# A message-passing layer on one core: which nodes a partition of a table step holds

## What is computed

```python
msg_in = concatenate([nodes[row], nodes[col], edge_features], axis=-1)
messages = relu(msg_in @ mW1 + mb1) @ mW2 + mb2
aggregated = segment_sum(messages, col, num_segments=12500)
upd = relu(concatenate([nodes, aggregated], axis=-1) @ uW1 + ub1) @ uW2 + ub2
y = nodes + upd
out = (y - mean(y)) / sqrt(var(y) + 1e-5)     # over the 64 features
```

## Time and profile before

| | us |
|---|---|
| Median of three runs | 2034.05 (2033.94 to 2034.74) |
| The profiled execution's own time | 2035.36 |
| Its span in the trace | 2033.6 |

### The profile page before, as it was taken

How to read it: one execution, slowest core, us unless ns; L and a number is a source line. 1 busy time by engine, 2 the same in 40 slices (tenths; PEclk the granted TensorE clock), 3 DMA queues, 4 the chain that set the end, 5 groups by cost and what they waited for, 6 DMA issues and landing times.

```text
span 2033.6 us, 34717 instructions
## 1 busy us (share of the span) xinstructions
PE 1408.9 (69%) x10080; PEld 1283.7 (63%) x10080; DVE 872.2 (43%) x2225; ACT 557.6 (27%) x928; POOL 1488.3 (73%) x1576
## 2 busy tenths in 40 slices
PE   6777767666667676666766676767676767767775
PEld 6766666566666666666665565656665656656664
DVE  3543333333333333333334444444444444544444
ACT  4322222222222222222222232333233333333332
POOL 1777777777777777777777777777777777777774
PEclk8876777777777877787777877887787788787877
DMA  9732223322322322232222322323232323322321
GB/s 233 226 87 78 78 77 81 80 77 78 81 77 78 82 79 77 78 81 80 77 77 72 80 79 76 80 77 81 77 80 78 80 75 81 79 78 75 82 80 43
DMA packets 167906, 173.50 MB, mean 85 GB/s; under 512 B 65718, under 2 KB 129497, under 8 KB 167785
## 3 DMA queue, kind: packets, MB, share of 16 engines
q0 software_dynamic: 50016, 102.53, 19.4%
q1 hardware_dynamic: 104168, 63.40, 11.2%
q10 hardware_dynamic: 13698, 7.28, 1.6%
HBM read 156.74 MB, written 16.31 MB: 85 GB/s over the span
## 4 chain that ended last, share of the span: by engine, by line
POOL 69%; issue 24%; DMA 3%; PE 2%; POOLq 1%; DVE 0%; ACT 0%; SPq 0%; DVEq 0%; ACTq 0%
POOL ag L227 69%; DMA src_table<-ag 1%; PE bank L375 1%; DMA dst_table<-picks 1%; POOLq L213 0%; POOLq L224 0%; POOLq L785 0%; DMA xc<-x_t 0%; DMA dst_table<-hid 0%; PE bank L264 0%; PE bank L642 0%; PE bank L648 0%; PE bank L274 0%; DMA ag<-src_table,slot_idx 0%; DMA picks<-edge_t 0%
## 5 line engine op out<-in xcount | busy, mean ns | idle before, releaser
L227 POOL DMA_INDIRECT ag<-src_table,slot_idx x1563 | 1481.7, 948 | 521.5 <-issue 475.7
L274 PE MATMUL bank<-oh,hid 128*128 128x96 f32 x3128 | 532.5, 325 | 421.9 <-DVE xc L333 378.1
L274 PEld LDWEIGHTS bank<-oh,hid 128*128 128x128 f32 x3128 | 478.2, 234 | 481.0 <-ACT hid L295 428.4
L316 DVE TENSOR_TENSOR hid<-bank,ag 128x512 f32<-128x512 f32 x391 | 270.4, 692 | 897.0 <-DMA ag<-src_table,slot_idx 769.8
L264 PE MATMUL bank<-picked,picks 128*128 128x128 f32 x3128 | 583.2, 346 | 5.9 <-DMA picks<-edge_t 5.4
L295 ACT ACTIVATE hid<-hid 128x512 f32<-128x512 f32 x391 | 245.8, 629 | 1175.0 <-DVE hid L316 1175.0
L264 PEld LDWEIGHTS bank<-picked,picks 128*128 128x128 f32 x3128 | 521.2, 252 | 9.5 <-issue 5.9
L289 ACT ACTIVATE picks<-bank 96x512 f32<-96x512 f32 x391 | 226.6, 580 | 173.6 <-PE bank L251 131.4
L303 DVE TENSOR_TENSOR oh<-iota,rel 128x384 f32<-128x384 f32 x391 | 217.8, 557 | 118.9 <-PE bank L278 64.2
L251 PE MATMUL bank<-ident_bf,oh 128*96 128x128 bf16 x1564 | 194.2, 261 | 53.3 <-DVE oh L303 52.7
L251 PEld LDWEIGHTS bank<-ident_bf,oh 128*96 128x96 bf16 x1564 | 147.8, 155 | 104.1 <-DVE oh L303 66.2
(11 more groups left out here) (57 smaller groups left out, 327.8 us busy)
## 6 DMA issues: line engine op xcount, KB each, us to landing
picks<-edge_t SPq DMA_DIRECT2D x391, 64.0 KB
ag<-src_table,slot_idx POOLq DMA_INDIRECT x1563
picked<-dst_table SPq DMA_DIRECT2D x391, 48.0 KB
src_table<-ag SPq DMA_DIRECT2D x25, 256.0 KB, 4.2
dst_table<-picks SPq DMA_DIRECT2D x17, 256.0 KB, 4.6
xc<-x_t ACTq DMA_DIRECT2D x8, 400.0 KB, 15.3
resid<-x_rows SPq DMA_DIRECT2D x24, 128.0 KB
out<-resid ACTq DMA_DIRECT2D x24, 128.0 KB
```

What stands on the lines that cost most here:

```text
L227: pool.indirect_dma_start(out=ag[:, k, j * DH:(j + 1) * DH], out_offset=None, in_=src_table, in_offset=bass.IndirectOffsetOnAxis(ap=slot_i ...
L274: nc.tensor.matmul(ps_a[q][:, 0:WIN], hid[:, q, j * DH:(j + 1) * DH], oh[:, r, j * WIN:(j + 1) * WIN], start=(j == 0), stop=(j == TPG - 1))
L316: dve.tensor_tensor(hid[:, q, :], ps_h[q][:, :], ag[:, k, :], ALU.add).then_inc(s_pre, 1)
```

## The change

A step's rows in memory are the same 512 as before, but they are dealt out otherwise. Before, partition p of block b held node 128 b + p of the step, and its 128 values went to a row of its own. Now it holds node 4 p + b, so that the four blocks of partition p are four rows in a row. For that the stationary operand of block b is every fourth column of the step, from column b on, a step of 16 bytes in `xc`; and `table_rows` names the rows in the new order. Also, PE now waits for the parts of x of the whole step ahead of its first matmul, not block by block.

```diff
--- before.py
+++ after.py
@@ -356,23 +356,24 @@
 
         def table_rows(table, n):
 
-            return table[n * TB * P:(n * TB + step_blocks(n)) * P, :].rearrange("(b p) n -> p b n", p=P)
+            return table[n * TB * P:(n * TB + step_blocks(n)) * P, :].rearrange("(p b) n -> p b n", p=P)
 
         def pe_table(s_mm, s_cp, w):
 
             pe = nc.tensor
             for n in range(TSTEPS):
                 wait(pe, s_cp, n - 3)
-                for b in range(step_blocks(n)):
-                    at = (n * TB + b) * P
-                    if w is w_src:
-                        for part in sorted({at // XP, (at + P - 1) // XP}):
+                nb, at = step_blocks(n), n * TB * P
+                columns = xc[:, at:at + nb * P].rearrange("k (p b) -> k b p", b=nb)
+                for b in range(nb):
+                    if w is w_src and b == 0:
+                        for part in sorted({at // XP, (at + nb * P - 1) // XP}):
                             pe.wait_ge(s_xt[part], 16)
                             if part % 2 == 0:
                                 pe.wait_ge(s_zero_dve, part // 2 + 1)
                             else:
                                 pe.wait_ge(s_zero_pool, part // 2 + 1)
-                    last = nc.tensor.matmul(banks[n % 4][:, b * DH:(b + 1) * DH], xc[:, at:at + P],
+                    last = nc.tensor.matmul(banks[n % 4][:, b * DH:(b + 1) * DH], columns[:, b, :],
                                             w[:, :], start=True, stop=True)
                 last.then_inc(s_mm, 1)
```

## The result

| | before | after |
|---|---|---|
| Median of four runs, us | 2034.39 (2033.94 to 2036.25) | 2054.88 (2053.49 to 2056.0) |
| Ratio | | 1.0099 (1.0081 to 1.0116) |
| The profiled execution's span | 2033.6 | 2053.0 |
| First gather | 52.9 | 59.3 |

The kernel is 20.5 us slower, where 2028.3 was forecast. The time is above the range, and of the times named ahead of it rival A's 2048.5 is the nearest.

The account below looks back on a forecast made before the run. The gathers on POOL bound the kernel, starting once the source table is in memory. First gather at 28 + 17.7 + 1.4 = 47.1 us, 5.8 sooner than 52.9, took the median from 2034.05 to 2028.3 us; range 2024.0 to 2036.5.

Parts of the forecast that it names:

- rival A: PE's weight loads: the 16-byte step doubles them, 1.71 us a step, a wait opens on L322, 2048.5 us; 17 in 100.
- The frame: POOL's line of gathers: time is the first gather's start plus a constant, as long as no other wait opens.
- Part 5: PE's stationary operand: reading it with a 16-byte step was costed at nothing, as PE has time.
- Part 4: Line of gathers stays closed: index copy (L322) comes at 80.5, wanted at 87.2; slack before was 7.2 us.
- Part 1: Stores 0 to 3 beside the load of x: land between 13 and 26 us, store 4 moves at 28 (27 to 30).
- Part 2: Source stores 4 to 24: 5.7 MB with bases at 322 GB/s, 17.7 us (14.4 to 19.7).
- the sum: First gather's start: 28 + 17.7 + 1.4 = 47.1 us, 5.8 sooner than 52.9; bounds 42.8 to 51.1.
- rival B: Table stores: pieces cheaper in number only, either not joined (2034) or bytes count (290 GB/s, 2030.3 us); 21 in 100.

Follow-up runs that it names:

- source_only_2: The changed kernel with its new row order and 16-byte operand step for the source table only, target table as before; 2041.61 us, ratio 1.0033.
- rows_only_2: The changed kernel's 2 KB store pieces, but the stationary operand read contiguously, so table rows are permuted against their nodes; 2031.55 us, ratio 0.9983.
- pairs_2: The changed kernel with two pairs of neighbouring nodes per partition: 1 KB store pieces, 8-byte operand step; 2033.83 us, ratio 0.9998.
- source_rows: The kernel before with 2 KB source table pieces, contiguous operand, and source indices turned into row numbers by DVE; 2033.41 us, ratio 0.9994.
- the probe: The kernel before with the target table's matmuls replaced by sixteen per step at varied operand steps, f32 and bf16; 0.056 to 0.238 us a pass.
- rows_small_late: rows_only_2's kernel with the loads of w_dst, b_rows and picked issued behind source stores 0 to 3; 2030.16 us, ratio 0.9978.
- small_late: The kernel before with only the loads of w_dst, b_rows and picked moved behind source stores 0 to 3; 2035.86 us, ratio 1.0006.

## Why the prediction was wrong, point by point

*The frame was right, within some us.* The time is the first gather plus a constant as long as no wait opens in the line: source_only_2 has a first gather 5.9 us later and takes 6.9 us more, rows_only_2 one 3.5 sooner and takes 3.2 less. In the traces the span less the first gather is 1980.7 us before, 1980.1 to 1981.7 in rows_only_2, source_only_2, pairs_2 and source_rows, but 1982.2 to 1986.3 in the five later ones, so that the constant is one to about 6 us. The wait it named as the one to open, on L322, is the one that opened.

*Part 5 failed, the operand at nothing, and with it the choice between the forecast and rival A.* The load's pass takes 0.233 us and not 0.112, so PE's two tables are 93 us of work and not 45, and PE had no such time to spare: it is that which cost 20.5 us. What the rows had was the pace of f32 columns that lie side by side, 0.112 us for 128 or 0.9 ns a column; that it leaves time for a step was the author's estimate and not shown, and at 16 bytes the probe has 0.233 us, 1.8 ns a column. The transposes, taken as the nearest row, were no evidence: they are bf16 with 4 bytes from column to column, where the probe shows no extra cost either (0.056 us), and they say nothing of 16 bytes. The text called the part its weakest and named the price from which it decides (0.175 us a load); with no row between 4 and 16 bytes, 17 in 100 was little.

*Rival A, the slower load, was right, its size a little small.* It took 1.71 us a step, the pace before at a granted clock of 0.50; it is 1.87, 0.233 a load. Its sum gave the first gather at 55.1 (59.3), the target table at 100.9 (106.0) and 14.4 us of loss (20.5). With 1.87 the same sum is 13.67 + 22 x 1.87 + 0.9 + 2.9 = 58.6, and 56.7 + 25 x 1.87 + 4.9 = 108.4 for the target table, whose landings were quicker than the 4.2 us taken. Its rule for the loss was right: the copy at 112.2 where 93.0 was wanted before is 19.2 us, against the 19.4 between the spans.

*Part 4 held.* It gave 7.2 us of slack and the rule by which it is used up. In rows_only_2 the gathers start 3.5 us sooner and no wait opens; source_only_2 has a target table 5.1 us later (84.4 for 79.3) behind a first gather 5.9 later, and has 0.6 us of waits on L322.

*Part 1 was wrong in what q1's packets are.* That q1 and x's queue send one for one held, in count: 194 and 195 in the earlier trace rows, 601 and 592 from 9 to 25 us, 160 and 160 in rows_small_late. But in the first two, most of q1's were small loads' pieces, not stores'. The earlier trace rows couldn't tell the two apart, since w_dst, b_rows and picked go in 512-byte pieces as the stores did; SP's own order, with six small loads ahead of the first store, could. A packet of x has 6400 bytes, not some 5 KB; the mean is lower for the 4-byte packets between (152 of 6400 bytes and 43 of 4 in the earlier trace rows). So with 2 KB rows the first landing that ScalarE waits for comes at 28.4 in rows_only_2, and ScalarE still stops:

```profile
28.37 1.14 ACT L387 ACTIVATE ag<-bank 128x512 f32<-128x512 f32 x2 [6.19 <-DMA src_table<-ag]
```

The prediction also left out a wait: SP's read-back of the bases stands between store 9 and store 10 and waits for the four base stores. Before, SP was too late to notice (34.04, right behind store 9). In rows_only_2 stores 4 to 9 are issued by 29.86, and SP stands 3.6 us:

```profile
21.11 8.75 SPq L405 DMA_DIRECT2D src_table<-ag  x6
33.50 0.34 SPq L810 DMA_DIRECT2D resid<-window_base_f  x1
...
34.80 10.08 SPq L405 DMA_DIRECT2D src_table<-ag  x15
```

*Part 2 was mis-sized the other way.* Taken were 322 GB/s. Measured, from 36 to 40 and from 40 to 44 us: 368 and 386 in rows_only_2, 400 and 393 in rows_small_late, where before there are 276 and 291.

```profile
DMA packets 825, 1.47 MB, mean 368 GB/s; under 512 B 93, under 2 KB 147, under 8 KB 825
```

```profile
DMA packets 1960, 1.10 MB, mean 276 GB/s; under 512 B 73, under 2 KB 1960, under 8 KB 1960
```

Part 2 also had PE out of the way, as 13 steps in under 12 us. They begin only when ScalarE goes on, and at first at a low clock (0.56 from 36 to 38 us in source_rows): there the 13 go from 32.69 to 46.98, and they are what the start waits for.

The two errors partly cancel, which is luck: from part 1 the start is later than forecast, from part 2 sooner, and rows_only_2's 49.4 is within the 42.8 to 51.1 of the sum. Of rival B, the half in which the pieces aren't joined is refuted by the packet counts, and the half in which bytes are what counts by these rates, though the earlier trace rows has 354 GB/s with 512 bytes; the 322 and 325 of source_rows say nothing of it, as PE paces them.

## What to carry to other kernels

An operand's step is a cost of its own: before you deal data out otherwise to make a transfer larger, ask in which unit the stepping lands, and price it on the engine that reads it, with the step, dtype and operand that it will have; here, in f32, 8 bytes were nearly free (0.116 us for 0.112) and 16 doubled the load (0.233). Before you take a queue's packets for a transfer's, list what else was issued on that queue ahead of it, with the size of its pieces. When a transfer has become faster, look which engine feeds it: here PE's 0.89 us a step took over as the bound. And recompute the slack behind the first bound for each rival: the same slower load cost 6.9 us where only one table had it, and 20.5 where the second used up the slack.

## What the runs showed of the hardware

- An f32 matmul's operand, stationary or moving, with 16 bytes or more from column to column takes 0.22 to 0.24 us for 128 columns, instead of 0.112; with 12 bytes 0.173, with 8 bytes 0.113 to 0.116. At 16 bytes it is the same at both levels of the clock, 1.88 us a step around 0.50 and 1.87 at 1.00, where before it took 1.71 and 0.90.
- A bf16 stationary operand is nearly free of it (0.062 at 16 bytes, 0.063 at 32), a bf16 moving one is not (0.116 at 8 bytes, 0.228 at 16, for 0.056).
- Stores of 2 KB pieces keep the sixteen engines as busy as those of 512 bytes and move more: at 36 to 40 us q1 takes 99.7% of them for 1.47 MB in rows_only_2, and took 98.4% for 1.10 MB before. In source_rows, with 2 KB too, it is 98.4% for 1.29 MB, and from 40 to 44 us 86.7% for 1.30 MB, where PE paces them.
- While x was loaded, q10 and q1 sent equal numbers of packets, with small packets on q1 (191 and 192, 0.97 and 0.08 MB, from 15 to 20 us in the changed kernel) as with larger ones (160 and 160, 0.82 and 0.29 MB, from 17 to 21 in rows_small_late). With the 320 packets of w_dst, b_rows and picked ahead of the first store its landing came 7.5 us later (28.4 in rows_only_2, 20.9 in rows_small_late). At x's end the counts part: 50 and 136 before, from 25 to 26 us.
- In one series of runs the kernel before took 2602.7 us instead of 2034, with POOL waiting 535 to 562 us on DVE's index copies in the four variants traced there, and a mean granted clock of 0.70 for 0.79. A slower chip isn't shown: these runs have the same chip number as the later ones of small_late and rows_small_late, where the kernel before took 2034.8. The cause is open.
